# Gathers paced by landed gathers, and a group's second layer on VectorE moved into the next group but one

## The reference

```python
msg_s = (s_n @ Ws_src)[src] + (s_n @ Ws_dst)[dst]
msg_v = (v_n x Wv_src)[src] + (v_n x Wv_dst)[dst]
w1 = rbf @ W_rbf
m1_s, m1_v = _cg_tp(msg_s, msg_v, y0, y1, w1 ...)      # first layer: products with harmonics y, dot, cross
a = leaky(m1_s @ W_alpha) . alpha_dot                  # attention logits, softmax over the edges of a dst
val_s = m1_s @ Ws_val
val_v = (m1_v x Wv_val) * sigmoid(val_s @ Wg)
m2_s, m2_v = _cg_tp(sigmoid(val_s), val_v, y0, y1, w2 ...)   # second layer
h = [m2_s @ Ws_vlin, m2_v x Wv_vlin]                   # heads, stored per edge
agg = segment_sum(softmax(a) * h, dst)
```

## Time and profile before

| | |
|---|---|
| median of 3 runs | 9591.08 us (9548.35 to 9623.26) |
| the profiled execution | 9599.6 us |
| span of its instructions | 9597.3 us |
| first edge pass in it | about 240 to 5950 us |

### The profile page before, as it was taken

How to read it: one execution, slowest core, us unless ns; L and a number is a source line. 1 busy time by engine, 2 the same in 40 slices (tenths; PEclk the granted TensorE clock), 3 DMA queues, 4 the chain that set the end, 5 groups by cost and what they waited for, 6 DMA issues and landing times. The chain is left out here.

```text
span 9597.3 us, 196058 instructions
## 1 busy us (share of the span) xinstructions
PE 7798.3 (81%) x43972; PEld 6155.8 (64%) x43973; DVE 6800.5 (71%) x16742; ACT 5176.7 (54%) x16950; POOL 5019.7 (52%) x5222
## 2 busy tenths in 40 slices
PE   5788888888878888888888887898788887887778
PEld 3677777777767777767777776897444444444446
DVE  7667667767767666676677777787777776776677
ACT  5455555555545555555555554113666666666665
POOL 1555555555545555555555553784366665565650
PEclk7777777777777777787777878999899999999999
DMA  7333222222222222222222222677444443443435
GB/s 242 74 77 76 78 75 77 77 77 78 78 68 78 77 75 75 76 79 75 74 78 78 77 76 59 220 223 153 116 113 114 111 112 104 110 112 107 111 105 174
DMA packets 971876, 968.06 MB, mean 101 GB/s; under 512 B 452750, under 2 KB 788750, under 8 KB 971662
## 3 DMA queue, kind: packets, MB, share of 16 engines
q0 software_dynamic: 225792, 385.65, 16.4%
q1 hardware_dynamic: 512032, 346.40, 13.0%
q10 hardware_dynamic: 233936, 234.90, 7.4%
HBM read 677.57 MB, written 288.65 MB: 101 GB/s over the span
## 5 line engine op out<-in xcount | busy, mean ns | idle before, releaser
L745 POOL DMA_INDIRECT e_g_dst<-table_dst,e_idx x1568 | 1495.5, 954 | 1695.2 <-ACT logits L898 1324.1
L784 PE MATMUL e_ps_t<-ident,e_m 128*128 128x128 f32 (+1 forms) x7840 | 1499.7, 334 | 687.0 <-issue 307.2
L745 POOL DMA_INDIRECT e_g_src<-table_src,e_idx x1568 | 1497.4, 955 | 988.6 <-issue 608.2
L2021 POOL DMA_INDIRECT f_e<-table,f_src x1568 | 1492.0, 952 | 980.8 <-issue 521.8
L784 PEld LDWEIGHTS e_ps_t<-ident,e_m 128*128 128x128 f32 (+1 forms) x7840 | 1128.0, 170 | 891.6 <-issue 598.8
L2078 PE MATMUL f_ps_a<-sums 128*128 128x384 f32 x3936 | 1514.7, 531 | 1.5 <-DVE sums L2178 1.5
L877 ACT ACTIVATE e_m1t<-e_ps_t 128x512 f32<-128x512 f32 (+1 forms) x1176 | 688.0, 598 | 950.2 <-remote 393.6
L2078 PEld LDWEIGHTS f_ps_a<-sums 128*128 128x128 f32 x3936 | 763.3, 204 | 569.7 <-issue 216.7
L2067 PE MATMUL f_ps_w<-f_w,f_hidden 64*128 64x192 f32 x3936 | 491.9, 372 | 494.1 <-DVE sums L2178 242.3
L1004 DVE TENSOR_TENSOR e_vy<-e_msg,e_ps_w 128x384 f32<-128x384 f32 x392 | 216.7, 553 | 817.4 <-ACT e_ps_w L957 513.2
L896 ACT ACTIVATE e_ps_v<-e_ps_v 128x128 f32<-128x128 f32 x392 | 102.7, 262 | 1284.4 <-remote 726.7
(11 more groups left out here) (268 smaller groups left out, 17900.8 us busy)
## 6 DMA issues: line engine op xcount, KB each, us to landing
edge_values<-e_h ACTq DMA_DIRECT2D x392, 330.0 KB
r_h<-edge_values SPq DMA_DIRECT2D x196, 660.0 KB, 4.0
sums<-sums ACTq DMA_DIRECT2D x492, 192.0 KB
e_g_src<-table_src,e_idx POOLq DMA_INDIRECT x1568
e_g_dst<-table_dst,e_idx POOLq DMA_INDIRECT x1568
f_e<-table,f_src POOLq DMA_INDIRECT x1568
f_rbf<-basis SPq DMA_DIRECT2D x492, 48.0 KB
basis<-t_part SPq DMA_DIRECT2D x42, 448.0 KB, 3.1
```

Of the source, the lines that this page charges most:

```text
L745: pool.indirect_dma_start(out=into[:, r, t, :], out_offset=None, in_=table, in_offset=bass.IndirectOffsetOnAxis(ap=idx[:, r, c:c + 1], axi ...
L784: last = nc.tensor.transpose(ps_t[bank][0:channels, t * P:(t + 1) * P], rows(t), ident[:])
L2021: pool.indirect_dma_start(out=rows_of_units[:, (place * RING + r) * T + t, :], out_offset=None, in_=table, in_offset=bass.IndirectOffsetOn ...
```

## The change

Three things. (1) The gathers have three semaphores in place of one: `from_src` for the first three of `g_src`, `from_dst` for the first three of `g_dst`, `fourths` for the fourth of either. The four of `g_dst` now also wait until the first three of `g_src` of the same group have landed, and the four of `g_src` until the first three of `g_dst` of the group before have landed. SP and VectorE wait for all three semaphores. (2) VectorE does the whole second layer of group u-2 in body u: the five operations that read `mix` stand among the message additions of group u, and the four short ones among the first layer's dot and cross products. Before, the five were done for group u-1 at the end of body u. (3) `heads_with_y(u-3)` and `heads_sum(u-3)` move behind the cross products, around `scalars_by_weights(u)`. The number of arithmetic operations for a group is the same.

```diff
             def load(u, r, i):
-                    wait(sp, gathered[r], i * 32 * T)
+                    wait(sp, from_src[r], i * 16 * (T - 1))
+                    sp.sem_inc(issued, 1)
+                    wait(sp, from_dst[r], i * 16 * (T - 1))
+                    sp.sem_inc(issued, 1)
+                    wait(sp, fourths[r], i * 32)
                     sp.dma_start(idx[:, r, :], idx_d[u]).then_inc(idx_in[r], 16)
...
                 wait(pool, first, (u - RING) * FIRST + MSG if not isinstance(u, int) or u >= RING else 0)
+                if not isinstance(u, int) or u > 0:
+                    pool.wait_ge(from_dst[(r - 1) % RING], (i + 1 if r else i) * 16 * (T - 1))
                 pool.sem_inc(issued, 1)
...
                         wait(pool, gated, u - RING)
+                    if side == 1:
+                        pool.wait_ge(from_src[r], (i + 1) * 16 * (T - 1))
                         pool.sem_inc(issued, 1)
...
-                        ).then_inc(gathered[r], 16)
+                        ).then_inc(landed[r] if t < T - 1 else fourths[r], 16)
...
             def message(u, r, i):
-                dve.wait_ge(gathered[r], (i + 1) * 32 * T)
+                dve.wait_ge(from_src[r], (i + 1) * 16 * (T - 1))
+                dve.wait_ge(from_dst[r], (i + 1) * 16 * (T - 1))
+                dve.wait_ge(fourths[r], (i + 1) * 32)
...
             def body(u, r, i):
-                v, w, x = u - 1, u - 2, u - 3
+                w, x = u - 2, u - 3
                 message(u, r, i)
+                mixed_with_y(w, (r - 2) % RING)
+                message_of_tile(r, 1)
+                mixed_sum(w)
+                message_of_tile(r, 2)
+                gated_vectors(w)
+                message_of_tile(r, 3)
+                gated_with_y(w)
+                products_with_y(u)
                 second_dot_of_two(w)
-                message_of_tile(r, 1)
+                dot_of_two(u)
                 second_cross_of_two(w)
-                message_of_tile(r, 2)
+                dot_of_three(u)
                 second_dot_of_three(w)
-                message_of_tile(r, 3)
+                cross_of_two(u)
                 second_cross_of_third(w)
-                products_with_y(u)
-                dot_of_two(u)
+                cross_of_third(u)
                 heads_with_y(x, rx)
-                dot_of_three(u)
-                cross_of_two(u)
+                scalars_by_weights(u)
                 heads_sum(x, rx, nx)
-                cross_of_third(u)
-                scalars_by_weights(u)
-                mixed_with_y(v, (r - 1) % RING)
                 vectors_by_weights(u)
-                mixed_sum(v)
                 cross_by_weights(u)
-                gated_vectors(v)
-                gated_with_y(v)
```

More of the change, by code:

```diff
@@ L625, in edges @@
                                                     sem("ones_set"))
-        idx_in, y_in, rbf_in, gathered = ([sem(f"{n}{r}") for r in range(RING)]
-                                          for n in ("idx_in", "y_in", "rbf_in", "gathered"))
+        idx_in, y_in, rbf_in, from_src, from_dst, fourths = ([sem(f"{n}{r}") for r in range(RING)]
+                                          for n in ("idx_in", "y_in", "rbf_in", "from_src", "from_dst", "fourths"))
         stored = [sem(f"stored{r}") for r in range(2)]
@@ L737, in gather @@
                 wait(pool, first, (u - RING) * FIRST + MSG if not isinstance(u, int) or u >= RING else 0)
+                if not isinstance(u, int) or u > 0:
+                    pool.wait_ge(from_dst[(r - 1) % RING], (i + 1 if r else i) * 16 * (T - 1))
                 pool.sem_inc(issued, 1)
-                for side, (table, into) in enumerate(((table_src, g_src), (table_dst, g_dst))):
+                for side, (table, into, landed) in enumerate(((table_src, g_src, from_src),
+                                                              (table_dst, g_dst, from_dst))):
                     if side == 1 and (not isinstance(u, int) or u >= RING):
                         wait(pool, gated, u - RING)
+                    if side == 1:
+                        pool.wait_ge(from_src[r], (i + 1) * 16 * (T - 1))
                         pool.sem_inc(issued, 1)
@@ L1146, in _ @@
             rounds(dve, body)
[L1147 to L1162, removed]
+            for w in (groups - 2, groups - 1):
+                mixed_with_y(w, w % RING)
+                mixed_sum(w)
+                gated_vectors(w)
+                gated_with_y(w)
+                second_dot_of_two(w)
+                second_cross_of_two(w)
+                second_dot_of_three(w)
+                second_cross_of_third(w)
+                x = w - 1
                 heads_with_y(x, x % RING)
                 heads_sum(x, x % RING, x // 2)
+            heads_with_y(groups - 1, RING - 1)
+            heads_sum(groups - 1, RING - 1, (groups - 1) // 2)
             leaky(groups - RING)
```

## The result

The changed kernel takes 9143.77 us, the median of 3 runs (9135.79 to 9155.26), against 9591.08 before: a ratio of 0.9538 with a 95% interval from 0.9476 to 0.9601. Forecast were 9165 us. The profiled execution has a span of 9134.0 us against 9597.3, 463 less.

The account below looks back on a forecast made before the run. Bound: POOL's rhythm of gather bursts and what it holds up in TensorE. Two bursts and pauses, 2 x 4.71 + 2.40 + 1.40 = 13.22, plus 0.20, give 13.42 us against 14.53: 434 us off 9599.6, about 9165; range 8870 to 9700.

Parts of the forecast that it names:

- misses: Groups where the third block's result misses the pause: 17.3 us long, 4.1 more; one in twenty gives 0.20 a group.
- The pause of 2.40: POOL's pause before the `g_dst` burst, ended by the gate; said to stay 2.40 us despite the second wait.
- The landed pause: POOL's new wait before `g_src` for landed gathers: at least 0.85 us, at most 2.40, taken as 1.40.
- 0.87 and 1.42 us of waits: VectorE's waits a group at `mixed_with_y` (0.87) and `heads_with_y` (1.42), which the new order should remove.
- the 0.67 of the long bursts: POOL's bursts run on without a pause: 14.53 - 13.86 = 0.67 us a group, some 260 us in all.
- the moved second layer: VectorE's body: second layer costs nothing in its new place; fourth message addition comes 0.7 us later, taken up by the pause.
- the pause of 0.99: POOL's pause in today's regular bursts, before the `g_src` burst: 0.99 us.
- The fourth rival: POOL: waits have mostly passed, long bursts stay with their 0.67; 14.09 us a group, about 9430; chance 0.06.
- the moved heads: VectorE's heads behind the cross products: ScalarE's `keep` and store come later, only store and harmonics loading queue behind; costed at nothing.
- The third rival: Pause too short for the third block: such groups take 17.3 us; with half of them 9885 us; chance 0.14.
- The first: Gathers do not hold TensorE: a group takes TensorE's 12.0 us, the kernel 8610; chance 0.08.
- The second rival: VectorE's waits only move, back before `products_with_y`: 4.37 us there, 14.5 a group, about 9600; chance 0.16.

Follow-up runs that it names:

- four landed gathers: The changed kernel with both pauses waiting for all four gathers of a burst in place of three: 9689.53 us, ratio 1.0174.
- the pauses alone: The changed kernel's three semaphores and both added waits, with VectorE's body and tail of the kernel before: 9210.56 us, ratio 0.9624.
- the order alone: The kernel before, its gathers and one semaphore kept, with VectorE's body and tail of the changed kernel: 9806.89 us, ratio 1.0219.
- the two runs with bursts of two: The changed kernel with two gathers a burst, middle tiles left out: 8170.79 us; or with all gathers as four bursts of two: 9890.87 us against 10020.04.
- half the gathers: The changed kernel with two gathers in place of four in each first-pass burst, middle tiles' rows staying zero: 8170.79 us, ratio 0.8576.
- two landed gathers: The changed kernel with both pauses waiting for two landed gathers in place of three: 9522.21 us, ratio 0.9996.

## Why the prediction was right

The total was right. Of the cause that it rested on, this much is borne out: POOL's gathers, run on without pauses, cost the pass its time. With both pauses the gain is there in the main, with one, or with waits that have passed, it is lost. That results are held when they fall due late in a burst is borne out for `mix` and `values`, but `heads` came at once in the run of four landed gathers. Several terms of the sum were off, and they cancelled; that the total came within 0.3% is in part luck.

**The cycle.** Forecast were two bursts, 9.42 together, pauses of 2.40 and 1.40, and 0.20 for misses: 13.42 us. Measured are 9.65, 2.06 and 1.64: 13.35. The bursts are longer because some gathers are (mean 995 ns in place of 955 for the source rows). The pause of 2.40 was called what stays; it is the pause of an ordinary group, but the mean of the pass was 3.42, and the whole gain is its fall to 2.06. The row was typical and not the mean. The landed pause was given a least value of 0.85; the common least is 1.1, so either a gather is known to have landed some 0.3 us later behind its issue than the slices of the earlier trace rows suggested, or POOL takes that much longer from there; the runs do not tell which.

**The parts.** Here the prediction failed most. It credited VectorE's order with the vanishing of 0.87 and 1.42 us of waits and the pauses with the 0.67 of the long bursts. That 0.67 was the distance of the mean from one pair of groups called ordinary, 13.86; the median group took 14.86 us (counted in the trace), so the pair was not the ordinary case. In the runs the pauses alone bring 3.8%, the order alone costs 2.2%, and on top of the pauses it brings about 1%. The step that failed is that of the moved second layer: it placed the fourth message addition within VectorE's body (0.7 us later) and not against POOL's burst, where it comes 1.9 us earlier, and so the order alone takes away the pause of 0.99. The fourth rival, the order without working pauses, was priced at 9430; it is slower than before.

**The waits.** `e_partial` went as said, 1.42 to 0.13 a group, `e_mixed_v` from 0.87 to 0.32 only. `e_vy` did not grow to 3 us; it stayed at 2.14. Missed was the wait at `logits`, 0.65 a group: of the moved heads the text said that only the store and the loading queue behind ScalarE's `keep`, but `leaky` on VectorE waits for `keep` too. It costs nothing that shows, as moving it showed.

**The third rival.** Groups of over 17 us were given one in twenty; there are 42 among 391, about as many as before (38) and twice what was allowed. Their price is met by 123 groups under 11.5 us, where 39 were before. Message additions 13.2 to 13.5 apart are right as a mean and wrong as a picture. The long waits went, as said: the longest of VectorE is 7.1 us, against 16.2.

**The first and second rivals.** If gathers did not hold TensorE's results, a group was to take TensorE's 12.0 us and the kernel 8610; it takes 13.38. Against this rival stand also the two runs with bursts of two, where the late results all but ended, and the order alone, where the bursts ran on and ScalarE's remote waits for the first layer's blocks doubled. The second rival, that the waits only move, holds for the order alone; with the pauses the wait before the products stayed at 2.14 us, not 4.37, and a group is not 14.5.

**What stays open.** In the groups where it can be told, it is the word of a result that comes late and not the result. What in the gathers delays it, and why `heads` was spared with four landed gathers, and with the order alone too (117 due more than 2.5 us into a burst, 0.04 us late in the median, counted in the trace), stays open. So does the part of the clock: over the pass it rose with the gain, from 0.78 to 0.83, and was 0.82 with the pauses alone, 0.76 with four landed gathers and 0.99 with half the gathers. Whether it is a cause of the gain or comes with it, no run tells apart.

## What to carry to other kernels

A wait that is meant to pace a queue paces it only if it is still unmet when the queue comes to it. Measure the condition's time against the queue's own, not against the body in which it is set; and pace both sides, for with one the run-on here just moved to the other. Before crediting a rearrangement with the waits that it removes, ask which gap in another queue those waits were making.

## What the runs showed of the hardware

Results of TensorE that fell due more than 2.5 us into a burst of four gathers were mostly announced late, about 1 us behind the end of a burst (median): 213 of 214 of `mix` in the kernel before, 82 of 83 of `values` with four landed gathers and gaps of 2.4 us. Those due in a pause or in the first 1.25 us of a burst came at once, 169 of 174 and 147 of 147. With bursts of two and as many gathers 7 of 634 were late. Against it stands `heads` with four landed gathers, 237 due late in a burst and at once, and with VectorE's order alone, 117.

Behind a wait that POOL found unmet, the next gather started 0.81 us after what ended the wait (median before, the fourth message addition). Behind a wait that had passed, it followed 0.30 us behind the gather before it, as without a wait (two landed gathers).

The kernel before took 9505 us on one chip and 10020 on another, 5% apart, with a granted clock over the span of 0.835 on the one and 0.817 on the other (medians of the runs).
